# Expert choice in a fused decoder layer: logits and ranks out of PSUM by ScalarE, the choice in four steps

## The chip, the cores and the metric

One core of one Trainium2 chip runs the whole kernel. The metric is device time in microseconds (us) of one execution; the median of 3 runs before the change is 750.56 us (749.78 to 751.29).

## The reference, cut to what matters

The layer takes 64 sequences of 64 tokens, 128 wide, all float32, and adds three blocks one after the other, each on a layer norm of what came before:

```python
x = x + self_attention(layernorm(x))            # 16 heads of 8, causal
x = x + cross_attention_and_ffn(layernorm(x), ctx)
x = x + ffn_block(layernorm(x))                 # below
# ffn_block: h = x + rotary_attention(rmsnorm(x)); y = h + moe(rmsnorm(h))
logits = xf @ w_router                          # 4096 x 8
probs = softmax(logits); topw, topi = top_k(probs, 2)
topw = topw / sum(topw)
out = sum over the two chosen experts of topw * (silu(xf @ wg) * (xf @ wu)) @ wd
```

The change touches what lies between the logits and the sorted rows: for each token the first and the second best of 8 experts, their two weights, and the row of each (token, expert) pair in an array sorted by expert.

## The kernel before, in words

**Jobs.** The 4096 tokens are 8 tiles of 512, each of 4 sub-tiles of 128 (`SUB`). Each tile goes through three kinds of job, SELF, CROSS and ROTARY, in an order given by `JOBS` (line 123): 24 jobs, of which the ROTARY ones are jobs 11, 14, 16, 18, 20, 21, 22 and 23. A job is four slots, one for each pair of sequences, written (n, p) below. `walk` (line 185) is the order of the work on every engine. In slot (n, p) come, in this order:

- scores (TensorE, L950 and L962) and their shift by the row maximum (VectorE, `shift_scores`, L1145 the maximum, L1149 the subtraction) for the *next* slot;
- the steps of the first half slot, "place 0";
- `attend` (TensorE, L990) and `normalise` (VectorE, L1159 and L1161) for the slot before;
- the transposes of the shifted scores (TensorE, L974) and the exponentials (ScalarE, L1019) of (n, p);
- the steps of the second half slot, "place 1".

**Steps.** What surrounds attention is cut into named steps, and `STEPS` (line 131) lists by hand, for a job n+away, in which slot and half slot of job n each stands. Away 2 and 1 are steps before the job's attention (st, ap: norm; xT, q, k, v: transposes and projections, qr and kr their rotated halves), -1 those behind it (oT, wo, h0, h1, ff, and for ROTARY st2, ap2, hT), -2 and -3 the routing of a ROTARY job: `lg` (logits), `rk` (ranks) and `s0` to `s3`, the moves of the four sub-tiles. Each engine walks the same list and does its own part of each step, strictly in that order; where two jobs have steps in one half slot, the one with the lower away comes first. What is left after the last job is in `last_steps` (line 168).

**The routing before.** `lg`: TensorE makes the logits (L921, slot 0, place 1 of job n-away). VectorE's `choose_dve` (line 444) waits for them, copies them out of PSUM (L453), and chooses in a chain of dependent small instructions (L457 to L463: maximum, less than it, index or 8, first index, one-hot, for both choices), gives the logit gap (L465) and sums up choices (`carried`, L466 to L469). `rk`, one slot later: TensorE sums ranks (L925, L926) once `sel_ready` is there; ScalarE turns the gap into a weight (L1071); VectorE's `place_dve` (line 475) reads the ranks from PSUM (L482), makes row numbers and weights (L485 to L494), and releases the moves by `rows_known`. Each move is two indirect DMAs issued by GpSimd (L1331), which also runs the norm factors (`layer_norm`, `rms`, L1272), the two rotary sums (L1339 for kr, L1341 for qr) and two passes of ap2 (L1322, L1325), all in one queue.

**PSUM.** All these products go through a ring of four banks (`BANKS`). The use number c of a bank, counted over steps, transposes and attends in the order of `walk`, waits until use c-4 has been drained (`free`, line 867), so an engine that copies a bank out late holds up TensorE four uses later. The names of uses are in `count_uses` (line 219).

**The expert stage.** After the last step VectorE makes tables (`tables_dve`), and 71 blocks of 128 sorted rows go through the experts. SyncE loads the first block only after all moves have landed (`rows_moved`, line 555).

## Time and profile before

| | |
|---|---|
| median of 3 runs | 750.56 us |
| the profiled execution | 752.07 us, its span 750.3 us |
| mean granted TensorE clock | 0.915 of full speed |
| attention stage, 28 to 534 us of the span | 24 jobs of 4 slots |
| moves and tables alone, 534 to 568 us | GpSimd issues 22 of the 64 indirect DMAs |
| experts and the sum, 568 us to the end | 71 blocks |

The spans of a busy engine say little here: TensorE, VectorE, ScalarE and GpSimd hand work to each other in every slot. The time line has for each entry its start in us, its length in us, engine, line, operation, output and inputs, the count of instructions merged, and in brackets how long the engine sat idle before and what released it. A slot is best told by VectorE: L1145 is the first instruction of each, so a window from one of its starts to the next is one slot.

### The profile page before, as it was taken

How to read it: one execution, taken by the hardware profiler on the slowest of the kernel's cores; microseconds unless marked ns; L12 is line 12 of the kernel's file. 1: busy time of each engine (PE TensorE's matmuls, PEld its weight loads, DVE VectorE, ACT ScalarE, POOL GpSimd, SP SyncE). 2: the span in 40 equal slices, each digit the busy share in tenths (PEclk: the TensorE clock that was granted, in tenths of full speed). 3: DMA queues.
4: the chain of work that ended last, by engine and by line, in shares of the span. 5: the costliest groups of instructions: out<-in, count | busy, mean ns of one | idle time of the engine just before them, and what ended most of it. 6: DMA issues, size and time to landing. Idle time of an engine off the chain costs nothing.

```text
span 750.3 us, 28778 instructions
## 1 busy us (share of the span) xinstructions
PE 617.3 (82%) x11859; PEld 465.6 (62%) x11859; DVE 504.5 (67%) x1165; ACT 376.8 (50%) x742; POOL 250.4 (33%) x361
## 2 busy tenths in 40 slices
PE   3798999999989879988879679687525999999960
PEld 2465766766656656655546446455425999999960
DVE  3377687777777876876777567477652666666645
ACT  4254566556655536464544424423243777667730
POOL 6010110101121324423633442425771444444440
PEclk9599999999999989999999889898756999999995
DMA  4304600001001000100100000000022222222219
GB/s 127 109 18 137 174 18 18 28 17 42 3 21 37 3 26 32 42 17 17 42 19 27 16 23 24 16 17 31 30 64 53 56 69 66 63 65 62 65 51 325
DMA packets 44960, 38.88 MB, mean 52 GB/s; under 512 B 11248, under 2 KB 37424, under 8 KB 44832
## 3 DMA queue, kind: packets, MB, share of 16 engines
q1 hardware_dynamic: 40512, 28.11, 12.7%
q0 software_dynamic: 4320, 8.92, 3.5%
q8 instruction: 97, 1.59, 0.9%
q14 instruction: 31, 0.25, 0.1%
HBM read 18.71 MB, written 12.01 MB: 41 GB/s over the span
## 4 chain that ended last, share of the span: by engine, by line
PE 60%; DVE 17%; issue 7%; POOL 7%; DMA 4%; ACT 4%; SPq 1%; DVEq 0%; POOLq 0%; ACTq 0%
PE ps_s L615 12%; PE ring L937 7%; PE ring L974 7%; PE ps_s L962 6%; DVE rmax L1145 5%; PE ring L623 5%; PE ring L990 5%; DVE shifted L1149 5%; POOL moved_dram L1331 3%; PE ring L860 3%; PE ps_s L950 3%; PE ring L851 3%; PE ring L913 2%; PE ring L917 2%; PE ring L910 2%
## 5 line engine op out<-in xcount | busy, mean ns | idle before, releaser
L1145 DVE TENSOR_REDUCE rmax<-ps_s 128x16 f32<-128x1024 f32 x96 | 117.2, 1221 | 80.3 <-PE ps_s L962 79.9
L1019 ACT ACTIVATE probsT<-ring 128x512 f32<-128x512 f32 x192 | 104.9, 595 | 123.3 <-PE ring L974 123.1
L1149 DVE TENSOR_TENSOR shifted<-ps_s,rmax 128x1024 f32<-128x1024 f32 x96 | 117.6, 1225 | 10.3 <-PE ring L990 0.5
L974 PE MATMUL ring<-const,shifted 128*128 128x128 f32 x768 | 109.1, 286 | 2.7 <-DVE room L1221 2.6
L615 PE MATMUL ps_s<-room 128*128 128x128 f32 x852 | 108.9, 279 | 0.0
L615 PEld LDWEIGHTS ps_s<-room 128*128 128x128 f32 x852 | 102.9, 196 | 0.0
L582 POOL DMA_INDIRECT y_dram<-room x71 | 68.0, 957 | 94.8 <-DVE room L701 92.1
L990 PEld LDWEIGHTS ring<-vbd,probsT 128*32 128x32 f32 x6144 | 64.5, 112 | 55.7 <-issue 53.3
L974 PEld LDWEIGHTS ring<-const,shifted 128*128 128x128 f32 x768 | 85.4, 145 | 7.5 <-DVE room L1221 3.4
L692 DVE SCALAR_TENSOR_TENSOR room<-room,ps_s 128x384 f32<-128x384 f32 x71 | 39.3, 554 | 59.8 <-ACT room L665 59.8
L990 PE MATMUL ring<-vbd,probsT 128*32 128x18 f32 x6144 | 75.0, 188 | 3.7 <-issue 2.6
L653 ACT ACTIVATE room<-w_exp 128x768 f32 x71 | 59.7, 843 | 29.8 <-issue 24.9
L1272 POOL TENSOR_TENSOR pt<-mv,small 128x4 f32<-128x4 f32 x24 | 4.8, 200 | 198.5 <-DVE mv L1174 198.5
L1331 POOL DMA_INDIRECT moved_dram<-moved,pos_i x64 | 62.6, 978 | 24.3 <-issue 15.9
L962 PE MATMUL ps_s<-room,qT 32*64 32x256 f32 x1536 | 68.5, 414 | 2.2 <-DVE shifted L1149 2.2
L623 PE MATMUL ring<-w_exp,room 128*128 x426 | 59.2, 276 | 0.9 <-DVE room L701 0.9
L623 PEld LDWEIGHTS ring<-w_exp,room 128*128 128x128 f32 x426 | 53.3, 192 | 1.1 <-issue 1.1
L937 PE MATMUL ring<-xT,w_f 128*128 128x512 f32 x64 | 37.7, 673 | 13.4 <-ACT xT L1083 10.2
L1058 ACT ACTIVATE vbd<-ring 64x512 f32<-64x512 f32 x48 | 30.4, 633 | 35.1 <-PE ring L860 34.8
L695 DVE TENSOR_TENSOR room<-room,ps_s 128x384 f32<-128x384 f32 x71 | 39.3, 554 | 7.3
L1221 DVE TENSOR_TENSOR room<-ring,const 128x512 f32<-128x512 f32 x32 | 22.0, 686 | 26.5 <-PE ring L937 26.5
L962 PEld LDWEIGHTS ps_s<-room,qT 32*64 32x64 f32 x1536 | 23.0, 134 | 26.9 <-issue 23.7
(159 smaller groups left out, 897.7 us busy)
## 6 DMA issues: line engine op xcount, KB each, us to landing
room<-kS SPq DMA_DIRECT2D x96, 64.0 KB, 1.9
room<-moved_dram SPq DMA_DIRECT2D x71, 65.0 KB
room<-y_dram SPq DMA_DIRECT2D x16, 256.0 KB, 5.7
room<-in_x SPq DMA_DIRECT2D x8, 256.0 KB, 3.5
out<-room SPq DMA_DIRECT2D x8, 256.0 KB, 6.1
cin<-in_ctx SPq DMA_DIRECT2D x8, 192.0 KB, 2.8
w_exp<-in_L_ffn_wg SPq DMA_DIRECT2D x1, 1536.0 KB, 8.6
w_exp<-in_L_ffn_wu SPq DMA_DIRECT2D x1, 1536.0 KB, 11.9
```

What stands on the lines that cost most here:

```text
L582: G.indirect_dma_start(out=y_dram, in_=yb[r], in_offset=None, out_offset=bass.IndirectOffsetOnAxis(ap=xb[r].bitcast(I32)[:, E:E + 1], axis ...
L615: last = mm(bank[r][:, k * P:(k + 1) * P], w, xbT[r], start=True, stop=True)
L623: last = mm(y_bank[r], hh[r][:, k * P:(k + 1) * P], weights(e, W_DOWN + k * E, E), start=(k == 0), stop=(k == HC - 1))
L653: nc.scalar.activation(w_held[c % HELD], w, ACT.Copy).then_inc(w_copied, 1)
L937: last = mm(ps_g[:], w, (cT if kind == CROSS and name == "k" else xT)[:], start=True, stop=True)
L962: last = mm(ps_s[SEQ * b:SEQ * b + SEQ, g], qT[r][some, tok:tok + SEQ], kbd[r][some, :, tok:tok + SEQ], start=not causal, stop=True)
L974: last = nc.tensor.transpose(ring[u.bank][:, k * P:(k + 1) * P], flat[:, c:c + P], ident)
L990: last = mm(ring[u.bank][rows, c:c + 2 * (D + 1)], probsT[p % 2][:, k, rows], vbd[r][:, at:at + 2 * (D + 1)], start=True, stop=True)
L1019: nc.scalar.activation(probsT[p % 2][:, 4 * g:4 * g + 4, :], ring[u.bank][:].rearrange("p (k c) -> p k c", c=P), ACT.Exp, scale=SCALE)\
L1145: V.reduce_max(rmax[p % 2][:].rearrange("p (g k) -> p g k", g=GROUPS), ps_s, AX.X).then_inc(rmax_ready, 1)
L1149: V.tensor_tensor(shifted[p % 2][:].rearrange("p (g k) s -> p g k s", g=GROUPS), ps_s, rmax[p % 2][:].rearrange("p (g k) -> p g k", g=GROU ...
L1331: G.indirect_dma_start(out=moved_dram, in_=moved[t % 2][:, k, s, :], in_offset=None, out_offset=bass.IndirectOffsetOnAxis(ap=pos_i[t % 2][ ...
```

## The change

The choice is taken apart and moved. `lg` and `rk` are now drained by ScalarE, with a copy into SBUF each (`logits`, `rank`, the latter one row of 8 longer in the last tile), and VectorE no longer reads either bank. VectorE's part becomes four steps: `c0` (`choose_dve`: four `max` instructions that give the 8 sorted logits of a sub-tile each, gap, not equal, index or 8), `c1` (`hot_dve`: the one-hot rows of both choices), `c2` (`carry_dve`: sums) and `pl` (`place_dve`). They stand in slot 1 place 0 (c0), slot 1 place 1 (c1, c2) and slot 3 place 0 (pl); `rk` goes from slot 1 to slot 2. The moves go later: s0 from slot 2 to slot 3, s1 from slot 3 to slot 0 of the next job, s2 and s3 from slot 1 place 1 to slot 0 place 1 and slot 1 place 0 of that job. `last_steps` is ordered anew.

```diff
@@ -140,13 +140,14 @@
          ROTARY: (((), ()), (("oT",), ("wo", "st2")), ((), ("ap2",)), ((), ("hT",)))},
     -2: {SELF: (((), ()), ((), ()), ((), ()), ((), ())),
          CROSS: (((), ()), ((), ()), ((), ()), ((), ())),
-         ROTARY: (((), ("lg",)), ((), ("rk",)), ((), ("s0",)), ((), ("s1",)))},
+         ROTARY: (((), ("lg",)), (("c0",), ("c1", "c2")), ((), ("rk",)), (("pl",), ("s0",)))},
     -3: {SELF: (((), ()), ((), ()), ((), ()), ((), ())),
          CROSS: (((), ()), ((), ()), ((), ()), ((), ())),
-         ROTARY: (((), ()), ((), ("s2", "s3")), ((), ()), ((), ()))},
+         ROTARY: ((("s1",), ("s2",)), (("s3",), ()), ((), ()), ((), ()))},
 }
 MOVES = ("s0", "s1", "s2", "s3")
-NOT_ON_PE = ("st", "ap", "ap3", "st2", "ap2") + MOVES
+CHOICE = ("c0", "c1", "c2")
+NOT_ON_PE = ("st", "ap", "ap3", "st2", "ap2", "pl") + CHOICE + MOVES
 
 
 def steps_at(n, p, place):
@@ -168,18 +169,20 @@
 def last_steps():
 
     last = N_JOBS - 1
-    yield "lg", last - 1
-    yield "s2", last - 2
-    yield "s3", last - 2
+    for name in MOVES[1:]:
+        yield name, last - 2
     yield "oT", last
     yield "wo", last
-    yield "rk", last - 1
+    yield "lg", last - 1
     yield "st2", last
     yield "ap2", last
-    for name in MOVES:
+    for name in CHOICE + ("rk", "pl"):
         yield name, last - 1
-    for name in ("hT", "lg", "rk") + MOVES:
+    for name in ("hT", "lg") + CHOICE + ("rk", "pl"):
         yield name, last
+    for n in (last - 1, last):
+        for name in MOVES:
+            yield name, n
 
 
 def walk(steps, scores, shift, attend, exps):
@@ -322,9 +325,10 @@
     ones = sb("ones", [P, P])
     warm = sb("warm", [P, 1])
     logits = sb("logits", [P, SUB, EXPERTS])
-    top = sb("top", [P, 2, SUB])
+    top = sb("top", [P, SUB, EXPERTS])
+    other = sb("other", [P, 2, SUB, EXPERTS])
+    keyed = sb("keyed", [P, 2, SUB, EXPERTS])
     first_at = sb("first_at", [P, 2, SUB])
-    less, keyed, second = [sb(name, [P, SUB, EXPERTS]) for name in ("less", "keyed", "second")]
     chosen = sb("chosen", [P, 2, SUB, EXPERTS])
     sel = sb("sel", [P, SUB, EXPERTS])
     carried = sb("carried", [P, SUB + 1, EXPERTS])
@@ -333,7 +337,7 @@
     pos_i = [sb(f"pos_i{r}", [P, 2, SUB], I32) for r in range(2)]
     gap, w1st, wsum = [sb(name, [P, SUB]) for name in ("gap", "w1st", "wsum")]
     region_at = sb("region_at", [P, EXPERTS])
-    last_row = sb("last_row", [P, EXPERTS])
+    rank = sb("rank", [P, SUB + 1, EXPERTS])
     pad_at = sb("pad_at", [1, EXPERTS], I32)
     counts_i = sb("counts_i", [1, EXPERTS], I32)
     blocks_i = sb("blocks_i", [1, EXPERTS], I32)
@@ -441,28 +445,39 @@
         ins.then_inc(dve_chain, 1)
         dve.wait_ge(dve_chain, chain[0])
 
+    numbers = const[:, C_IOTA:C_IOTA + EXPERTS].unsqueeze(1).broadcast_to([P, SUB, EXPERTS])
+
+    def per_expert(x):
+        return x.unsqueeze(2).broadcast_to([P, SUB, EXPERTS])
+
     def choose_dve(dve, n):
 
         V, t, u = nc.vector, TILE_OF[n], used("lg", n)
-        iota = const[:, C_IOTA:C_IOTA + EXPERTS].unsqueeze(1).broadcast_to([P, SUB, EXPERTS])
-
-        def wide(x):
-            return x.unsqueeze(2).broadcast_to([P, SUB, EXPERTS])
-
-        dve.wait_ge(ring_filled, u.filled())
-        V.tensor_copy(logits[:], ring[u.bank][:, 0:SUB * EXPERTS].rearrange("p (s e) -> p s e", s=SUB))\
-         .then_inc(ring_drained[u.bank], 1)
         dve.wait_ge(ring_drained[u.bank], u.drained())
-        for k, src in enumerate((logits, second)):
-            in_turn(dve, V.reduce_max(top[:, k, :], src[:], AX.X))
-            in_turn(dve, V.tensor_tensor(less[:], src[:], wide(top[:, k, :]), ALU.is_lt))
-            in_turn(dve, V.scalar_tensor_tensor(keyed[:], less[:], float(EXPERTS), iota, ALU.mult, ALU.add))
-            in_turn(dve, V.tensor_reduce(first_at[:, k, :], keyed[:], AX.X, ALU.min))
-            in_turn(dve, V.tensor_tensor(chosen[:, k], iota, wide(first_at[:, k, :]), ALU.is_equal))
-            if k == 0:
-                in_turn(dve, V.scalar_tensor_tensor(second[:], chosen[:, 0], -1e30, logits[:], ALU.mult, ALU.add))
+        for s in range(SUB):
+            last = V.max(out=top[:, s, :], in_=logits[:, s, :])
+        in_turn(dve, last)
         wait(dve, weight_ready, t)
-        V.tensor_tensor(gap[:], top[:, 1, :], top[:, 0, :], ALU.subtract).then_inc(gap_ready, 1)
+        V.tensor_tensor(gap[:], top[:, :, 1], top[:, :, 0], ALU.subtract).then_inc(gap_ready, 1)
+        for k in range(2):
+            last = V.tensor_tensor(other[:, k], logits[:], per_expert(top[:, :, k]), ALU.not_equal)
+        in_turn(dve, last)
+        for k in range(2):
+            last = V.scalar_tensor_tensor(keyed[:, k], other[:, k], float(EXPERTS), numbers, ALU.mult, ALU.add)
+        in_turn(dve, last)
+
+    def hot_dve(dve, n):
+
+        V = nc.vector
+        in_turn(dve, V.tensor_reduce(first_at[:, 0], keyed[:, 0], AX.X, ALU.min))
+        in_turn(dve, V.tensor_tensor(chosen[:, 0], numbers, per_expert(first_at[:, 0]), ALU.is_equal))
+        in_turn(dve, V.scalar_tensor_tensor(keyed[:, 1], chosen[:, 0], float(EXPERTS), keyed[:, 1], ALU.mult, ALU.add))
+        in_turn(dve, V.tensor_reduce(first_at[:, 1], keyed[:, 1], AX.X, ALU.min))
+        in_turn(dve, V.tensor_tensor(chosen[:, 1], numbers, per_expert(first_at[:, 1]), ALU.is_equal))
+
+    def carry_dve(dve, n):
+
+        V, t = nc.vector, TILE_OF[n]
         V.tensor_copy(carried[:, 0, :], region_at[:] if t == 0 else carried[:, SUB, :])
         in_turn(dve, V.tensor_tensor(sel[:], chosen[:, 0], chosen[:, 1], ALU.add))
         for s in range(SUB):
@@ -475,13 +490,9 @@
     def place_dve(dve, n):
 
         V, t, u = nc.vector, TILE_OF[n], used("rk", n)
-        dve.wait_ge(ring_filled, u.filled())
-        rank = ring[u.bank][:, 0:SUB * EXPERTS].rearrange("p (s e) -> p s e", s=SUB)
-        if t == TILES - 1:
-            in_turn(dve, V.tensor_copy(last_row[:], ring[u.bank][:, SUB * EXPERTS:(SUB + 1) * EXPERTS]))
-        V.tensor_tensor(at_expert[:], chosen[:], rank.unsqueeze(1).broadcast_to([P, 2, SUB, EXPERTS]), ALU.mult)\
-         .then_inc(ring_drained[u.bank], 1)
         dve.wait_ge(ring_drained[u.bank], u.drained())
+        in_turn(dve, V.tensor_tensor(at_expert[:], chosen[:], rank[:, 0:SUB, :].unsqueeze(1)
+                                     .broadcast_to([P, 2, SUB, EXPERTS]), ALU.mult))
         in_turn(dve, V.reduce_sum(pos_f[:], at_expert[:], AX.X))
         r = t % 2
         wait(dve, rows_moved[r], MOVED * (t // 2))
@@ -496,8 +507,8 @@
     def tables_dve(dve):
 
         V = nc.vector
-        V.tensor_copy(pad_at[:], last_row[0:1, :]).then_inc(pads_known, 1)
-        in_turn(dve, V.tensor_scalar(counts_i[:], last_row[0:1, :], float(P - 1), None, ALU.add))
+        V.tensor_copy(pad_at[:], rank[0:1, SUB, :]).then_inc(pads_known, 1)
+        in_turn(dve, V.tensor_scalar(counts_i[:], rank[0:1, SUB, :], float(P - 1), None, ALU.add))
         in_turn(dve, V.tensor_scalar(blocks_i[:], counts_i[:], 7, None, ALU.logical_shift_right))
         in_turn(dve, V.tensor_copy(blocks_f[:, 3, :], blocks_i[:]))
         first = const[0:1, C_IOTA:C_IOTA + EXPERTS]
@@ -1066,10 +1077,22 @@
                 apply_rms(n)
             elif name == "ap3":
                 apply_third(n)
-            elif name == "rk":
-                act.wait_ge(gap_ready, TILE_OF[n] + 1)
-                nc.scalar.activation(w1st[:], gap[:], ACT.Exp).then_inc(weight_ready, 1)
-            if name in MOVES or name in ("st", "ap", "ap3", "st2", "ap2", "wo", "ff", "lg", "rk", "qr", "kr") or (kind == ROTARY and name in ("q", "k")):
+            elif name in ("lg", "rk"):
+                u, t = used(name, n), TILE_OF[n]
+                ps = ring[u.bank][:].rearrange("p (s e) -> p s e", e=EXPERTS)
+                if name == "lg":
+                    wait(act, sel_ready, t)
+                    act.wait_ge(ring_filled, u.filled())
+                    nc.scalar.activation(logits[:], ps[:, 0:SUB, :], ACT.Copy).then_inc(ring_drained[u.bank], 1)
+                else:
+                    wait(act, rows_known, t)
+                    act.wait_ge(ring_filled, u.filled())
+                    rows = SUB + 1 if t == TILES - 1 else SUB
+                    nc.scalar.activation(rank[:, 0:rows, :], ps[:, 0:rows, :], ACT.Copy)\
+                      .then_inc(ring_drained[u.bank], 1)
+                    act.wait_ge(gap_ready, t + 1)
+                    nc.scalar.activation(w1st[:], gap[:], ACT.Exp).then_inc(weight_ready, 1)
+            if name in MOVES or name in CHOICE or name in ("pl","st", "ap", "ap3", "st2", "ap2", "wo", "ff", "lg", "rk", "qr", "kr") or (kind == ROTARY and name in ("q", "k")):
                 return
             u = used(name, n)
             if name == "v":
@@ -1193,9 +1216,13 @@
                 u = used("wo", n)
                 dve.wait_ge(ring_drained[u.bank], u.drained())
                 stats_of(NORMS["st2", n], hres)
-            elif name == "lg":
+            elif name == "c0":
                 choose_dve(dve, n)
-            elif name == "rk":
+            elif name == "c1":
+                hot_dve(dve, n)
+            elif name == "c2":
+                carry_dve(dve, n)
+            elif name == "pl":
                 place_dve(dve, n)
             elif name in ("wo", "ff", "qr", "kr") or (kind == ROTARY and name in ("q", "k")):
                 u = used(name, n)
```

## Rows read from the trace of the kernel before

**Rows 1.** The page, part 1: busy time, share of the span, instructions of each engine.

```profile
PE 617.3 (82%) x11859; PEld 465.6 (62%) x11859; DVE 504.5 (67%) x1165; ACT 376.8 (50%) x742; POOL 250.4 (33%) x361
```

**Rows 2.** The waits, whole span: who waited for whom, us in total, times, longest.

```profile
PE ring L913 <- DVE at_expert L482: 10.3, 3, 3.5
...
DVE logits L453 <- PE ring L921: 10.5, 7, 7.1
...
PE ring L910 <- DVE at_expert L482: 7.7, 3, 3.3
```

**Rows 3.** Windows, slots (13,1) (16,1) (18,1) (20,0) (20,1) (21,1) (22,1) (23,1): us, busy us of each engine, PEclk, DMA share, GB/s.

```profile
274.55:283.11 8.56, 5.41 (x81) 4.52 (x84) 4.58 (x15) 1.63 (x5) 1.78 (x5) 0.60 0.01 2
...
339.98:346.71 6.73, 3.57 (x27) 0.99 (x28) 3.88 (x13) 1.84 (x6) 4.73 (x11) 0.75 0.00 0
...
386.82:392.71 5.89, 2.74 (x27) 0.95 (x28) 3.88 (x13) 1.71 (x6) 4.21 (x10) 0.87 0.00 0
...
431.19:441.17 9.98, 8.47 (x188) 5.57 (x188) 8.47 (x34) 3.06 (x6) 2.17 (x2) 1.00 0.08 29
...
441.17:449.76 8.59, 5.44 (x59) 3.01 (x60) 3.87 (x14) 2.35 (x6) 6.47 (x13) 0.60 0.05 17
...
466.67:472.04 5.37, 4.37 (x120) 3.53 (x112) 4.72 (x15) 2.30 (x5) 3.85 (x11) 1.00 0.02 5
...
497.20:505.20 8.00, 5.85 (x92) 4.90 (x96) 5.84 (x21) 1.76 (x5) 1.67 (x3) 0.79 0.00 0
...
519.39:526.75 7.36, 4.82 (x76) 3.37 (x80) 5.76 (x22) 0.30 (x2) 0.00 (x0) 0.60 0.04 11
```

**Rows 4.** Time line of slots 0 and 1 of job 20, VectorE and TensorE.

```profile
435.55 0.19 DVE L453 COPY logits<-ring 128x32 f32<-128x32 f32 x1 [0.72 <-PE ring L921]
...
438.61 0.77 DVE L469 TENSOR_TENSOR carried<-carried,sel 128x8 f32<-128x8 f32 x4
...
441.17 1.19 DVE L1145 TENSOR_REDUCE rmax<-ps_s 128x16 f32<-128x1024 f32 x1
...
443.88 0.29 DVE L1161 TENSOR_TENSOR att<-ring,rden 128x128 f32<-128x128 f32 x1
...
444.32 2.05 PE L913 MATMUL ring<-oT,w 128*128 128x512 f32 x2 [3.25 <-DVE at_expert L482]
...
445.15 0.17 DVE L494 TENSOR_TENSOR moved<-w1st,moved 128x4 f32<-128x4 f32 x1
```

**Rows 5.** Prices: time line of job 20; then instruction groups of VectorE and ScalarE by form.

```profile
440.87 0.38 DVE L1174 BATCH_NORM_AGGREGATE mv<-stats 128x2 f32<-128x6 f32 x4
...
L461 DVE TENSOR_TENSOR chosen<-const,first_at 128x32 f32<-128x32 f32 x16 | 3.1, 192 | 0.6
...
L1125 ACT ACTIVATE bias_qk<-ps_s 128x2 f32<-128x2 f32 x1 | 0.2, 172 | 0.1
```

**Rows 6.** Time line of job 18's end and job 19, GpSimd and ScalarE.

```profile
403.86 1.27 POOL L1339 TENSOR_TENSOR kS<-room 128x512 f32<-128x512 f32 x1 [7.08 <-DVE room L1221]
...
408.97 1.27 POOL L1341 TENSOR_TENSOR qT<-room 128x512 f32<-128x512 f32 x1 [3.84 <-DVE room L1221]
...
419.07 0.95 POOL L1331 DMA_INDIRECT moved_dram<-moved,pos_i  x1 [0.30 <-issue]
...
422.01 1.28 ACT L1049 ACTIVATE moved<-hres,rstd 128x128 f32<-128x128 f32 x4 [3.54 <-POOLq L1277]
```

**Rows 7.** Time line of job 14, GpSimd and TensorE.

```profile
295.71 0.20 POOL L1272 TENSOR_TENSOR pt<-mv,small 128x4 f32<-128x4 f32 x1 [4.53 <-DVE mv L1174]
...
302.69 0.60 PE L851 MATMUL ring<-const,xh 128*128 128x128 f32 x4
```

**Rows 8.** Time line of the last moves, GpSimd.

```profile
526.92 0.19 POOL L1272 TENSOR_TENSOR pt<-mv 128x4 f32<-128x4 f32 x1 [7.78 <-DVE mv L1174]
...
545.49 1.06 POOL L1331 DMA_INDIRECT moved_dram<-moved,pos_i  x1 [0.18 <-issue]
...
564.51 0.96 POOL L1331 DMA_INDIRECT moved_dram<-moved,pos_i  x1 [0.30 <-issue]
```

## The prediction

> **What bounds the kernel now.** I read the page first, then the waits, then slot by slot the time line. TensorE is busy for 82% of the span and VectorE for 67% [rows 1], but neither is simply the limit: the question is who waits in the slots that hold the choice. The waits name it. TensorE stood for 18.0 us in six places ahead of the first product behind oT (L913 and L910), and VectorE for 10.5 us ahead of its copy of the logits [rows 2]. The time line of job 20 shows how they hang together. VectorE waits 0.72 us for the logits, and from 435.55 to 439.38 it does nothing but the choice (3.83 us). So the next row maximum starts only at 441.17, the normalisation behind it ends at 444.17, and TensorE, which needs that normalisation's bank for h0, has stood for 3.25 us [rows 4]. The releaser printed is the read of ranks (L482); by its place in the bank count h0 waits for L1161, which ended 0.15 us before h0 began. After the stall the clock is down: PEclk is 0.60 in slot (20,1), and the two passes of L913 take 2.05 us [rows 3, 4]. Slots (20,0) and (20,1) take 9.98 and 8.59 us; slot (21,1), which has no choice but the same kind of work, takes 5.37 [rows 3].
>
> A second limit is GpSimd. In job 19 it runs norm factors from 410.2 on, then four indirect DMAs to 420.0, and ScalarE waits 3.54 us for the factors behind them [rows 6]. A third is the end: sixteen DMAs in one unbroken row, the first at 545.49, the last at 564.51, so 1.27 us each, and the experts start behind the last [rows 8].
>
> **The change, part by part.**
>
> *The choice itself.* Twelve dependent instructions of VectorE ahead of the sums, about 0.22 us apart (192 ns busy each, and the hand-over) [rows 5], and the gap, become: four max, gap, two unequal, two index-or-8, then five dependent ones. No row shows a max. Four independent small instructions, bn_aggr, took 0.38 us together [rows 5]; four dependent ones 0.77 us [rows 4]. I take 0.4, since the four max are independent too, and keep 0.8 as the upper end; less than 0.4 I exclude, as they are issued one by one. Then c0 is 0.4 + 0.4 + 0.3 = 1.1 us, c1 5 x 0.22 = 1.1, c2 1.1 as now. Together 3.3 us against 3.83, and the wait for the logits moves to ScalarE, where the copy has a nearest row of 172 ns from PSUM [rows 5] and is covered by that engine's idle time (2.35 us busy of the 8.59 of slot (20,1)) [rows 3].
>
> The Trainium skill (VectorE: DVE Perf Modes, section on the TRN2 errata) speaks against four small max: an operation from SBUF pays a fixed latency between instructions, so many small tiles pay it each time; by its formula (N+151)/0.96 ns, four of 8 elements in a row would be an estimated 0.66 us, and the sum below smaller by some 1.6 us. The trace disagrees for bn_aggr, whose 0.38 us leave 95 ns for each.
>
> *Where it stands.* Slot 0 loses the whole block. In job 20 the next maximum can then start when its scores and the stats ahead of it are done, by my working at 438.5, 2.7 us earlier than 441.17 [rows 4]; the same working gives 2.55 for job 13, 2.35 for 22, 2.9 for 16, 18 and 23. Slot 1 gains c0 ahead of the normalisation and c1, c2 behind it, and loses the placing (1.2 us, from the end of L1161 at 444.17 to that of L494 at 445.32). Maximum, shift and normalisation take 3.0 us (441.17 to 444.17) [rows 4], with a hand-over 3.1; + 1.1 + 2.2 makes 6.4. VectorE is busy in slot (13,1) 0.7 us longer than in (20,1), where it adds wo, and in (22,1) 2.0 longer, for hres and its stats [rows 3]. So slot 1 becomes 7.1 in job 13 (8.56 now), 6.4 in 16, 18 and 20 (6.73, 5.89, 8.59), 8.4 in 22 and 23 (8.00, 7.36) [rows 3]. With slot 0 that is 4.0 us for job 13, 3.2 for 16, 2.4 for 18, 4.9 for 20, 1.95 for 22 and 1.9 for 23.
>
> That holds where VectorE is last. h0 or wo no longer shares a bank with the normalisation, as the ranks' use of the ring has gone one slot on: it starts right behind the transposes; v, one use later, still waits. In 16 and 18 TensorE, late and at a lowered clock (PEclk 0.75 and 0.87) [rows 3], was behind VectorE at the next job's scores and gains more, 4.0 and 3.95. In 20 the ranks and xT, now ahead of these scores on TensorE, limit it to 3.3, in 13 the copies of xh and cT on ScalarE to 3.5. **Gain 3.5 + 4.0 + 3.95 + 3.3 + 1.95 + 1.9 = 18.6 us.**
>
> *pl in slot 3, place 0.* Eight instructions, 1.2 us, now stand ahead of the drains of ff and k or of a normalisation; q or kr waits for these banks. By the distance of the uses, 0.85 in job 13, 0.9 in 16, 0.7 in 18, 0.6 in 22; in job 20 0.35, the rest hidden in the wait for factors that follows anyway. **Cost 3.4.**
>
> *The moves in GpSimd's queue.* s1 and s2 (four DMAs, 5.1 us) now stand ahead of qr and of the norm factors of st, in jobs 14, 17, 19 and 21, and only s3 between these and st2. In job 19 GpSimd idles 3.84 us ahead of qr [rows 6], which takes up most of it; the factors come some 2.5 us later, but st2's come where they were, as its queue holds six DMAs and less idle time in place of four, and ScalarE's wait of 3.54 us [rows 6] stays. So 17, 19 and 21 cost nothing beyond what is counted. In job 14 there is no qr and the moves start only after pl: six DMAs at 1.27, 7.6 us, from about 291.5 (my estimate for the end of pl) to 299.1, against a start of the factors at 295.71; the transposes of xT at 302.69 [rows 7] slip by 2.25 us, of which 0.85 was counted. **Cost 1.4.** SyncE's queue has no move in it and keeps its order. Between nothing and the full 5.1 us a job I keep both ends for the range.
>
> *The end.* s1(21) to s3(21) start when pl(21) is done, at about 529.3, as now at 529.7, and GpSimd stays full from there; st2(22), from which that chain hangs (526.92) [rows 8], is earlier by the 1.9 counted. ScalarE copies the ranks of job 22 behind ap2(23), so its rows are known 0.8 us after GpSimd is ready for them. The choice of job 23 is some 2 us ahead of its moves and costs nothing. **Cost 0.8.**
>
> **Sum:** 18.6 - 3.4 - 1.4 - 0.8 = 13.0 us. The profiled execution took 752.07 us, 1.77 outside its span, so it would be 739.1; it lies 1.51 above the median, so the forecast for the median is **737.6 us**. A measurement of this kernel can tell about 0.2%, 1.5 us.
>
> **The rivals.**
>
> *A, half is given back.* The factors of st come 2 to 3 us late in four jobs, ScalarE waits in its own order in front of the exponentials, and TensorE behind these. For it: ScalarE already waited for factors in job 19 [rows 6]. Against it: two of the four jobs have ScalarE busy until then. At 1.6 us in four jobs: 13.0 - 6.4 = 6.6, so 744.0 us.
>
> *B, the stall in front of st2 shrinks as well.* If the earlier moves fill the gap ahead of qr (3.84) [rows 6] and TensorE's clock, once held up, stays up through slots 1 and 2, then jobs 19 and 21 give about 1.5 us each and the clock 3 more: 731.6 us.
>
> *C, slower: the queue of GpSimd.* Its place is slot 0 of jobs 14, 17, 19 and 21; its price the whole of four DMAs, 5.07 us, if the rows become known too late to use the idle time. It decides when more than (13.0 + 1.4) / 4 = 3.6 us a job come through to TensorE; at 5.07 the sum is 13.0 + 1.4 - 20.3 = -5.9, so 756.5 us. Against it: the idle time of 3.84 to 4.53 us is there [rows 6, 7].
>
> *D, no change.* The change doesn't unload what TensorE waits for: c0 ahead of the normalisation and c1, c2 ahead of the drain of wo cost slot 1 what slot 0 gains. Then only the shorter choice counts, six times 0.5 = 3.0, less than the costs of 5.6 but within the accuracy of these; 751 us. Against it: the wait for L1161 is lifted from h0 and wo by the bank count alone.
>
> **How the numbers follow.** Forecast 0.47, A 0.24, B 0.14, C 0.08, D 0.07. The forecast's own spread is 3 us either way (0.4 us more for max in six jobs is 2.4; each job's gain to 0.5). The range runs from 731 (B) to 746 (A with the dearer max), leaving out C, D and a part of B. Faster by over 0.2%: 0.47 + 0.24 + 0.14 and a little of D, 0.86; the same 0.06; slower 0.08.
>
> **What would show it.** Right: slot 0 of jobs 13, 16, 18 and 20 shorter by 2.4 to 2.9 us; no wait of L913 or L910 for VectorE over 1 us; PEclk near 1 in slot 1; the last move starting some 13 us earlier than 564.51; four max in about 0.4 us. Wrong, by step: a wait of L1031 for GpSimd of several us in jobs 14 to 21 (A, C); L1049's wait of 3.54 us gone (B); slot 1 longer than 8.4 us, or wo still stalled (D); a gap in the last sixteen moves of more than 1 us.

## The result and the profile after

The changed kernel takes **742.76 us** (median, 739.68 to 746.7, 7 runs) where the kernel before, on the same chip, takes 750.57 (749.78 to 752.77, 7 runs). The ratio is 0.9895, interval 0.9867 to 0.9923: 7.8 us faster. The profiled execution took 740.64 us, its span is 738.8. A second set of the same kernel is `again` below. The forecast of 737.6 was on the right side and 5 us too low; 742.76 lies in its range of 731 to 746.

In the kernel after, a line of VectorE's slot code is 23 higher than before: the row maximum is L1168, the normalisation L1182 and L1184. h0 is L924, wo L921, v L871, the scores' first product L961, ScalarE's copies L1086 (logits) and L1091 (ranks), the moves L1358.

The page, part 1 (busy time, share, instructions), answers to [rows 1]: nearly the same work in 11.5 us less.

```profile
PE 611.1 (83%) x11859; PEld 464.1 (63%) x11859; DVE 503.0 (68%) x1172; ACT 379.6 (51%) x758; POOL 250.2 (34%) x361
```

The waits, whole span (who, for whom, us in total, times, longest), answer to [rows 2]:

```profile
POOL moved_dram L1358 <- DVE moved L505: 51.1, 7, 12.8
...
PE ring L871 <- DVE att L1184: 12.4, 8, 2.5
ACT moved L1060 <- POOLq L1304: 10.7, 6, 2.5
...
ACT xh L1042 <- POOLq L1304: 8.2, 3, 4.9
```

Of the 18.0 us of h0 and wo, 0.7 is left; v (L871) waits 12.4 us in shorter pieces, where before the change it waited 6.3. The first line is new in its size (0.3 us before): GpSimd stands for the placing of the rows (L505).

Windows of the same slots as [rows 3], (13,1) (16,1) (18,1) (20,0) (20,1) (21,1) (22,1) (23,1), same columns:

```profile
272.30:279.06 6.76, 4.27 (x91) 3.48 (x94) 6.21 (x27) 2.35 (x4) 1.78 (x5) 1.00 0.01 2
336.96:343.16 6.20, 5.86 (x170) 3.50 (x170) 5.65 (x24) 4.94 (x10) 2.28 (x8) 1.00 0.01 3
382.37:388.57 6.20, 5.86 (x170) 3.50 (x170) 5.65 (x25) 4.93 (x10) 2.30 (x8) 1.00 0.01 3
426.00:433.26 7.26, 6.60 (x170) 4.10 (x173) 5.27 (x14) 2.06 (x6) 2.17 (x2) 1.00 0.11 40
433.26:439.78 6.52, 4.35 (x95) 2.87 (x84) 5.71 (x27) 3.09 (x6) 3.59 (x10) 1.00 0.01 3
458.29:463.67 5.38, 4.38 (x121) 3.54 (x113) 4.72 (x16) 2.31 (x5) 4.34 (x10) 1.00 0.05 15
483.25:491.82 8.57, 6.96 (x215) 5.92 (x215) 7.53 (x33) 3.37 (x6) 1.09 (x1) 1.00 0.02 5
504.19:512.43 8.24, 6.38 (x184) 5.09 (x183) 7.55 (x33) 3.06 (x7) 4.72 (x5) 1.00 0.16 51
```

PEclk (the third figure from the end) is 1.00 in every one, where it was 0.60 to 0.87 in most of them before. VectorE is busy for 5.71 of the 6.52 us of slot (20,1), and TensorE waits for it there (below): VectorE now sets that slot.

The time line of slot (20,1) answers to [rows 4]:

```profile
433.26 1.19 DVE L1168 TENSOR_REDUCE rmax<-ps_s 128x16 f32<-128x1024 f32 x1
433.43 1.09 PE L985 MATMUL ring<-const,shifted 128*128 128x128 f32 x8
...
434.36 1.02 PE L924 MATMUL ring<-oT,w 128*128 128x512 f32 x2
...
435.70 0.36 DVE L458 MAX8 top<-logits 128x8 f32<-128x8 f32 x4
...
437.12 0.29 DVE L1184 TENSOR_TENSOR att<-ring,rden 128x128 f32<-128x128 f32 x1
...
437.56 1.15 PE L871 MATMUL ring<-w_f,xT 128*64 128x64 f32 x32 [2.17 <-DVE att L1184]
...
438.74 0.77 DVE L484 TENSOR_TENSOR carried<-carried,sel 128x8 f32<-128x8 f32 x4
```

h0 (L924) has no bracket: it starts right behind the transposes and takes 1.02 us, not 2.05. The wait is now in front of v, 2.17 us. The four max take 0.36.

The same clock of slots can be laid over both traces. All times are us, slots named as in the prediction:

| job | 13 | 16 | 18 | 20 | 22 | 23 | sum |
|---|---|---|---|---|---|---|---|
| slot 0, before | 9.98 | 8.48 | 8.48 | 9.98 | 8.72 | 6.69 | 52.3 |
| slot 0, after | 7.27 | 5.61 | 5.59 | 7.26 | 6.35 | 3.84 | 35.9 |
| slot 1, before | 8.56 | 6.73 | 5.89 | 8.59 | 8.00 | 7.36 | 45.1 |
| slot 1, after | 6.76 | 6.20 | 6.20 | 6.52 | 8.57 | 8.24 | 42.5 |
| slot 2, before | 4.47 | 4.15 | 4.98 | 4.18 | 3.75 | | 21.5 |
| slot 2, after | 5.35 | 4.54 | 5.41 | 4.92 | 4.41 | | 24.6 |
| slot 3, before | 3.74 | 6.01 | 6.01 | 6.35 | 3.75 | | 25.9 |
| slot 3, after | 4.11 | 7.60 | 6.88 | 7.22 | 4.12 | | 29.9 |

So slots 0 and 1 gave 19.05 us; slots 2 took 3.1 of it back and slots 3 took 4.1, together 7.2. Job 14's slots 0 and 2 took another 2.6. Slots (19,3) and (21,3), which hold the wait for the factors of st2, went from 12.04 to 9.69 and from 12.68 to 9.49: 5.5 more gained. Start-up and the other slots took 0.5. At the last slot VectorE is 14.3 us ahead.

Some 4 us of these are lost in the tail. GpSimd's time line there, answering to [rows 8]:

```profile
512.60 0.19 POOL L1299 TENSOR_TENSOR pt<-mv 128x4 f32<-128x4 f32 x1 [2.48 <-DVE mv L1197]
...
517.38 1.06 POOL L1358 DMA_INDIRECT moved_dram<-moved,pos_i  x1 [0.88 <-DVE moved L505]
...
535.14 1.06 POOL L1358 DMA_INDIRECT moved_dram<-moved,pos_i  x1 [3.60 <-DVE moved L505]
...
554.16 0.96 POOL L1358 DMA_INDIRECT moved_dram<-moved,pos_i  x1 [0.30 <-issue]
```

The head is 14.3 us earlier (526.92 to 512.60) and the last move 10.35. The gap of 3.60 us in front of s0(22) is nearly all of the difference. From there to the end 1.2 us came back.

### The profile page after: what moved, and what is told of

It is laid out like the page before. It is cut to its first block, busy times and chain, and to the rows that moved or that the text cites. A ratio compares the mean times of both kernels' runs of the same rounds, so it can differ in the third digit from the quotient of the medians.

```text
span 738.8 us, 28821 instructions
## 1 busy us (share of the span) xinstructions
PE 611.1 (83%) x11859; PEld 464.1 (63%) x11859; DVE 503.0 (68%) x1172; ACT 379.6 (51%) x758; POOL 250.2 (34%) x361
## 4 chain that ended last, share of the span: by engine, by line
PE 58%; DVE 16%; issue 11%; POOL 7%; ACT 4%; DMA 2%; SPq 0%; DVEq 0%; POOLq 0%; ACTq 0%
PE ps_s L626 13%; PE ring L985 7%; PE ring L948 7%; PE ring L634 6%; PE ps_s L973 6%; DVE rmax L1168 5%; PE ring L1001 5%; DVE shifted L1172 4%; POOL moved_dram L1358 3%; PE ring L871 3%; PE ring L862 3%; PE ps_s L961 2%; PE ring L928 2%; POOL rstd L1299 1%; PE ring L921 1%
## 5 line engine op out<-in xcount | busy, mean ns | idle before, releaser
L1168 DVE TENSOR_REDUCE rmax<-ps_s 128x16 f32<-128x1024 f32 x96 | 117.2, 1221 | 77.6 <-PE ps_s L973 77.0
L1358 POOL DMA_INDIRECT moved_dram<-moved,pos_i x64 | 62.6, 978 | 70.3 <-DVE moved L505 51.1
L1069 ACT ACTIVATE vbd<-ring 64x512 f32<-64x512 f32 x48 | 30.4, 633 | 30.5 <-PE ring L871 30.3
L973 PEld LDWEIGHTS ps_s<-room,qT 32*64 32x64 f32 x1536 | 22.7, 132 | 26.6 <-issue 23.4
```

The lines of the kernel that those rows point to most:

```text
L973: last = mm(ps_s[SEQ * b:SEQ * b + SEQ, g], qT[r][some, tok:tok + SEQ], kbd[r][some, :, tok:tok + SEQ], start=not causal, stop=True)
L1168: V.reduce_max(rmax[p % 2][:].rearrange("p (g k) -> p g k", g=GROUPS), ps_s, AX.X).then_inc(rmax_ready, 1)
L1358: G.indirect_dma_start(out=moved_dram, in_=moved[t % 2][:, k, s, :], in_offset=None, out_offset=bass.IndirectOffsetOnAxis(ap=pos_i[t % 2][ ...
```

## The experiments

Each ran beside the kernel before, whose median was 750.57 us in the first set (again, old_places, moves_late_pair, tail), 750.02 in the second (lump_slot0, lump_slot1, pl_slot2, pl2_tail) and 749.3 in the third (the rest). The intervals of the ratios are 0.2 to 0.4% wide to either side, so a difference of 2 us between two sets is not told apart from none. All edits are to the changed kernel unless another is named. The rows of `STEPS` and `last_steps` are all that most of them touch.

### again: the changed kernel once more

> The changed kernel once more, as it is. Its runs so far lie between 739.7 and 746.7 us, those of before between 749.8 and 752.8. Expected: a median of 742.8 within 1.5 us, again with a spread of several us. If the spread comes from the attention stage (one theory), the start of the last move in this trace differs from 554.2 us by as much as the time does from 740.6; if it comes from the expert stage (the other), the last move stays at 554.2 within 0.5 us and the rest differs.

741.48 us (738.99 to 742.29), ratio 0.9888 (0.9866 to 0.991). This is the number the others are held against. Its last move starts at 551.93, 2.2 us sooner than above, with 1.65 us less of time, so the difference does not come from the expert stage; but it doesn't come from the slots either: the very first row maximum starts at 26.32 and not at 28.45. The profile shows how far two executions of one kernel differ: slots (12,3) and (13,1) took 5.61 and 8.17 us, in the profile above 6.79 and 6.76, and slot (2,1), long before any routing, took anything from 4.9 to 10.4 us over these runs. A difference of 2 us between two single profiles means nothing unless its slot is named.

### old_places: copies and shorter choice, old places

```diff
-ROTARY: (((), ("lg",)), (("c0",), ("c1", "c2")), ((), ("rk",)), (("pl",), ("s0",)))
+ROTARY: (((), ("lg", "c0", "c1", "c2")), ((), ("rk", "pl")), ((), ("s0",)), ((), ("s1",)))
-ROTARY: ((("s1",), ("s2",)), (("s3",), ()), ((), ()), ((), ()))
+ROTARY: (((), ()), ((), ("s2", "s3")), ((), ()), ((), ()))
```

> ScalarE's copies of logits and ranks and the shorter choice (four max) as in the changed kernel, but every step in the half slot where it stood before (choice behind lg in slot 0, ranks and placing in slot 1, moves and the last steps as before). If the gain comes from where the steps stand, little is left: a choice shorter by 0.5 us in six jobs, less 0.2 us for the hand-over from ScalarE, 1 to 3 us in all, so 748 to 750 us, with L1145's equivalent wait and the stall of the first product behind oT back at about 3 us each. If it comes from the copies or the max themselves, 743 us.

748.34 us, ratio 0.997 (0.9951 to 0.9989). Slots (20,0) and (20,1) are 9.76 and 8.71 us, as before the change. In the old places the new instructions are worth 2.2 us (0.8 to 3.7 by the interval); the other 7 are the places.

### lump_slot0, lump0_rk2 and lump_slot1: the choice's place against the ranks' place

```diff
 # lump_slot0
+ROTARY: (((), ("lg", "c0", "c1", "c2")), ((), ("rk",)), ((), ()), (("pl",), ("s0",)))
 # lump0_rk2
+ROTARY: (((), ("lg", "c0", "c1", "c2")), ((), ()), ((), ("rk",)), (("pl",), ("s0",)))
 # lump_slot1
+ROTARY: (((), ("lg",)), (("c0", "c1", "c2"), ()), ((), ("rk",)), (("pl",), ("s0",)))
```

> The scores (lg) and all of the choice stand together in slot 0, place 1; ranks in slot 1, place 1; the planned positions (pl) and s0 stay in slot 3. Theory 1 (the gain comes from what slot 1 loses): slot 0 takes the 3.3 us of the choice behind its normalisation, where VectorE would have to wait for ScalarE's copy of the scores as well, and slot 1 of the six jobs loses another 1.1 us; the sum of both slots is the same or up to 1 us worse for each job: 742 to 748 us. Theory 2 (VectorE has room in slot 0, whose length PE and GpSimd set): each of the six jobs is another 0.5 to 1 us shorter, 735 to 738 us.

> lump_slot0 (757.1 us) with one edit: the ranks go from slot 1 to slot 2, so that one use of the ring fewer lies between the normalisation's bank and h0 or wo. In lump_slot0 TensorE waited 3.25 us ahead of h0 in slot 1 of job 20 for a normalisation that had no choice ahead of it. Theory 1 (the bank count makes h0 wait): h0 starts right behind the transposes, and v, one use later, takes over about 2.1 us of the wait at a higher clock; 1 to 2 us less in each of jobs 13, 16, 18, 20, 22: 747 to 752 us. Theory 2 (only VectorE's work ahead of the row maximum counts, the bank does not): 755 to 758 us.

> All of the choice (c0, c1, c2) stands in slot 1 ahead of the normalisation, as before the change; ScalarE keeps both copies out of PSUM, and the moves stay where the change put them. Theory 1 (the split pays because c1 and c2 no longer stand between PE's scores and the normalisation): c1 and c2 are 2.2 us of VectorE, so slot 1 of jobs 13, 16, 18, 20, 22 and 23 is as long as it was or up to 2 us longer than after the change, where the slot of 20 and 22 holds the wait for the second half's statistics and hides part of it. Six times 1 to 2 us, some of it given back in the tail: 5 to 9 us over the changed kernel, 746 to 750 us. Theory 2 (VectorE's total is what counts, its places do not): nothing is added and nothing taken away, so the time is the changed kernel's within 1 us, 740 to 743 us. The old_places run, with all of the change but the places, stood at 748.3, and does not tell the choice's places from those of the moves and of the ranks; this run does.

| kernel | choice in | ranks in | median us | slots 0 + 1 of six jobs |
|---|---|---|---|---|
| lump_slot0 | slot 0 | slot 1 | 757.13 | 51.0 + 47.7 |
| lump0_rk2 | slot 0 | slot 2 | 743.46 | 50.9 + 28.7 |
| changed (again) | slot 1, split | slot 2 | 741.48 | 35.9 + 43.8 |
| lump_slot1 | slot 1, ahead of the normalisation | slot 2 | 750.66 | 35.9 + 51.5 |

The first pair differs in the place of the ranks alone, and by 13.7 us. In lump_slot0 no choice stands in slot 1, yet h0 waits there as it did before the change. Its time line, slot (20,1), and then that of lump0_rk2:

```profile
449.00 0.29 DVE L1184 TENSOR_TENSOR att<-ring,rden 128x128 f32<-128x128 f32 x1
449.44 2.05 PE L924 MATMUL ring<-oT,w 128*128 128x512 f32 x2 [3.25 <-DVE att L1184]
```

```profile
440.88 1.02 PE L924 MATMUL ring<-oT,w 128*128 128x512 f32 x2
...
441.50 1.19 DVE L1168 TENSOR_REDUCE rmax<-ps_s 128x16 f32<-128x1024 f32 x1
...
444.23 0.29 DVE L1184 TENSOR_TENSOR att<-ring,rden 128x128 f32<-128x128 f32 x1
444.67 1.15 PE L871 MATMUL ring<-w_f,xT 128*64 128x64 f32 x32 [2.77 <-DVE att L1184]
```

In the second, h0 has started before VectorE's slot has begun (440.88 against 441.50), and only v waits. The kernel's own count of uses (`count_uses`) says why: with the ranks in slot 1, the fourth use ahead of h0 is the attend that the normalisation drains, and with the ranks gone it is oT; v comes behind the attend instead. The windows of slot (20,1), lump_slot0 first (length, busy times, PEclk):

```profile
446.28:455.15 8.87, 5.71 (x59) 3.01 (x60) 2.87 (x6) 2.71 (x8) 3.60 (x10) 0.62 0.01 2
```

```profile
441.50:446.88 5.38, 2.61 (x58) 1.59 (x58) 2.88 (x6) 1.87 (x4) 3.59 (x10) 1.00 0.00 0
```

TensorE's stand and the lowered clock go together: 0.62 with the wait of 3.25 us, 1.00 with 2.77 behind a busy h0. Theory 1 of lump0_rk2 was right in kind and low in size: 743.46 against 747 to 752, and h0's wait had cost more than the 1 to 2 us a job put on it: slots (16,1) and (18,1) fell by 3.2 to 3.3 us each. The ranks are not free where they went: the five slots 2 grew from 21.7 to 23.5 us. Both theories of lump_slot0 missed: 757.13 against at most 748, since neither counted the wait of h0 that came back.

With the ranks in slot 2, moving the choice from slot 0 to slot 1 only moves 15 us from one slot to the other, 79.7 against 79.8 in the sum, and the medians, 743.46 and 741.48 in different sets, are not told apart. What matters within slot 1 is what stands ahead of the normalisation. In lump_slot1 it is all of the choice:

```profile
443.26 0.77 DVE L484 TENSOR_TENSOR carried<-carried,sel 128x8 f32<-128x8 f32 x4
...
444.67 1.98 PE L871 MATMUL ring<-w_f,xT 128*64 128x64 f32 x32 [4.27 <-DVE att L1184]
```

v waits 4.27 us, then takes 1.98 us and not 1.15. That costs 2.4 to 3.8 us in (13,1), 3.6 in (20,1) and 1.6 in (22,1), and nothing in 16, 18 and 23. Together 8 to 9 us in three jobs, where theory 1 had 5 to 9 in six; theory 2 falls. So the move into slot 1 needs the split, or it costs 9 us; with the split it is even with leaving the choice in slot 0.

### copy_by_dve: VectorE copies the logits

```diff
-        dve.wait_ge(ring_drained[u.bank], u.drained())
+        dve.wait_ge(ring_filled, u.filled())
+        V.tensor_copy(logits[:], ring[u.bank][:, 0:SUB * EXPERTS].rearrange("p (s e) -> p s e", s=SUB))\
+         .then_inc(ring_drained[u.bank], 1)
+        dve.wait_ge(ring_drained[u.bank], u.drained())
...
-                    nc.scalar.activation(logits[:], ps[:, 0:SUB, :], ACT.Copy).then_inc(ring_drained[u.bank], 1)
```

> The changed kernel, but VectorE copies the logits out of PSUM, at the head of c0 in slot 1, place 0; ScalarE keeps the copy of the ranks. Theory 1 (ScalarE's copy is what allows the choice to stand a slot later): the bank of the logits is held until c0, and the fourth use behind it, the transposes of slot 1, waits for it. In job 20 they started at 433.4 and c0 at 435.7, so 2.3 us and more for each of six jobs, some of it behind the row maximum that is due in any case: 748 to 757 us. Theory 2 (the copy is only an instruction of 0.2 us that changes engines): six times 0.25 us over the changed kernel, 742 to 743.5 us.

742.05 us (740.32 to 744.6): not told apart from the changed kernel, as theory 2 had it. Yet the wait that theory 1 named is there, in slot (20,1):

```profile
438.94 0.18 DVE L457 COPY logits<-ring 128x32 f32<-128x32 f32 x1
...
439.27 1.84 PE L988 MATMUL ring<-const,shifted 128*128 128x128 f32 x8 [2.52 <-DVE logits L457]
...
442.75 1.16 PE L874 MATMUL ring<-w_f,xT 128*64 128x64 f32 x32
```

The transposes wait 2.52 us for the bank, and v (here L874) no longer waits: TensorE stands once in front of a VectorE that is late anyway. Slot (20,1) grew by 1.95 us, those of 16, 18 and 23 by 0.2 each. In this trace the tail gave as much back: from GpSimd's first factor of the tail to the last move it took 39.1 us, in the changed kernel 41.6. So the copy of the logits by ScalarE, by itself, has no effect that the medians show. The copy of the ranks was not tested alone.

### pl_slot2: the placing behind the ranks

```diff
-((), ("rk",)), (("pl",), ("s0",))
+((), ("rk", "pl")), ((), ("s0",))
```

> The planned positions (pl) go from slot 3, place 0, where they stand ahead of the normalisation, to slot 2, place 1, right behind the ranks. Theory 1 (pl in slot 3 costs what the slot tables showed: some 3.9 us less 2.0 for the moves in job 14, 1.6 to 2.0 in job 16, less in the others): the slots named become shorter by 1.5 to 2 us in jobs 13 and 16 and by 0.5 in 18, 20 and 22, and slot 2 of each grows by up to 0.6 us where VectorE waits for ScalarE's copy of the ranks: 2 to 4 us faster than the changed kernel, 737 to 739.5 us. Theory 2 (a wait for the copy of the ranks holds up the residual sum behind it in slot 2, as pl is now due right behind PE's ranks): 0.5 to 1.2 us more in each slot 2, no gain or a loss of up to 3 us, 741 to 745 us.

734.25 us, ratio 0.9801 (0.9766 to 0.9837): some 7 us faster than the changed kernel, and nearly 3 below theory 1's range. The slots 3 of the five jobs fall from 29.9 to 26.6 us, the slots 2 stay (24.6 and 24.8), and job 14 gets its 2.6 back. GpSimd's wait for the placing falls from 51.1 to 30.4 us. GpSimd and ScalarE from slot (13,3) into job 14, in the changed kernel and then here:

```profile
288.42 1.20 POOL L1358 DMA_INDIRECT moved_dram<-moved,pos_i  x1 [6.34 <-DVE moved L505]
...
295.95 0.21 POOL L1299 TENSOR_TENSOR pt<-mv,small 128x4 f32<-128x4 f32 x1
...
300.13 1.65 ACT L1042 ACTIVATE xh<-room,shift,rboth 128x128 f32<-128x128 f32 x4 [2.48 <-POOLq L1304]
```

```profile
282.30 1.20 POOL L1358 DMA_INDIRECT moved_dram<-moved,pos_i  x1 [2.07 <-DVE moved L505]
...
291.36 0.20 POOL L1299 TENSOR_TENSOR pt<-mv,small 128x4 f32<-128x4 f32 x1 [1.53 <-DVE mv L1197]
...
295.54 1.65 ACT L1042 ACTIVATE xh<-room,shift,rboth 128x128 f32<-128x128 f32 x4
```

The six DMAs (three moves) are as long in both; above, the factors start straight behind them and ScalarE waits, below they are done 1.53 us before the factors start.

### moves_late_pair and moves_half_up: where the moves stand

```diff
 # moves_late_pair
+ROTARY: (((), ("lg",)), (("c0",), ("c1", "c2")), ((), ("rk",)), (("pl",), ("s0", "s1")))
+ROTARY: (((), ()), ((), ("s2", "s3")), ((), ()), ((), ()))
 # moves_half_up, an edit to pl2_tail below
+ROTARY: (((), ("lg",)), (("c0",), ("c1", "c2")), ((), ("rk", "pl")), (("s0",), ("s1",)))
+ROTARY: ((("s2",), ("s3",)), ((), ()), ((), ()), ((), ()))
```

> As the changed kernel, but s0 and s1 both in slot 3 and s2, s3 in slot 1 place 1 of the next job as before, so that no move stands ahead of qr and of the norm factors. If the moves ahead of the factors cost more than they give (rival A of the prediction), the slots of job 14 (14,1 to 15,0: 18.6 us in the changed kernel, 16.7 before) get about 2 to 4 us shorter and nothing else longer: 739 to 741 us. If they also take work out of the wait for st2's factors in jobs 19 and 21, as the shorter slots (20,1) and (22,1) of the changed kernel suggest (9.7 and 9.5 us against 12.0 and 12.7), these grow by 2.4 to 3.2 us each and the sum is 743 to 746 us.

> pl2_tail (731.55 us) with every move a half slot or more earlier: s0 and s1 in slot 3, places 0 and 1, s2 and s3 in slot 0 of the next job, places 0 and 1. Theory 1 (moves cost where they stand ahead of something due in GpSimd's queue, and slot 1 of the next job, with the rotary sum and the factors of st2 behind it, is such a place): 729 to 731 us. Theory 2 (s0 directly behind pl holds GpSimd's queue until the rows are known, in slot 3, where the norm factors and the rotary sum of kr stand behind it): 1 to 2 us more in jobs 17, 19 and 21, 733 to 737 us.

moves_late_pair: 741.87 us, the changed kernel's time, between the two theories; both their slots are there. Job 14 got 2.0 us back, though pl still stands in slot 3, but slots (19,3) and (21,3) became 11.82 and 12.47 us against 9.69 and 9.49, so the early moves are what had shortened them. moves_half_up: **724.58 us** (721.83 to 725.43), ratio 0.9654 (0.9626 to 0.9682), 7.0 below pl2_tail; the same two slots are 6.21 and 6.16 us, in pl2_tail 9.91 and 10.44. Theory 1 was right in kind and 4 us too small. GpSimd, ScalarE and TensorE in job 19, pl2_tail and then moves_half_up:

```profile
401.84 1.28 POOL L1370 TENSOR_TENSOR qT<-room 128x512 f32<-128x512 f32 x1
...
408.05 1.04 POOL L1360 DMA_INDIRECT moved_dram<-moved,pos_i  x1 [0.89 <-POOL shift L1301]
...
412.36 1.28 ACT L1062 ACTIVATE moved<-hres,rstd 128x128 f32<-128x128 f32 x4 [2.12 <-POOLq L1306]
...
414.17 1.35 PE L950 MATMUL ring<-xT,w_f 128*128 128x512 f32 x2 [3.37 <-ACT xT L1108]
```

```profile
403.35 1.28 POOL L1370 TENSOR_TENSOR qT<-room 128x512 f32<-128x512 f32 x1
...
411.64 1.27 ACT L1062 ACTIVATE moved<-hres,rstd 128x128 f32<-128x128 f32 x4
...
413.45 1.12 PE L950 MATMUL ring<-xT,w_f 128*128 128x512 f32 x2 [1.14 <-ACT xT L1108]
```

From qr to ap2 it is 10.5 us with a move (two DMAs) between the two sets of factors, and 8.3 without, and ScalarE waits no more. TensorE's wait for the projection behind it falls by 2.2 us, and its granted clock, 0.83 in slot (19,3) and 0.67 in (21,3) of pl2_tail, is 1.00 in both slots here; neither theory had the clock.

### tail, pl2_tail and c0_early

```diff
 # tail: last_steps
     for name in MOVES[1:]: yield name, last - 2
+    yield "lg", last - 1
+    for name in CHOICE: yield name, last - 1
     yield "oT", last
     yield "wo", last
-    yield "lg", last - 1
+    yield "rk", last - 1
     yield "st2", last
     yield "ap2", last
-    for name in CHOICE + ("rk", "pl"): yield name, last - 1
+    yield "pl", last - 1
 # pl2_tail: pl_slot2 and tail together
 # c0_early: pl2_tail, and
+ROTARY: (((), ("lg", "c0")), ((), ("c1", "c2")), ((), ("rk", "pl")), ((), ("s0",)))
```

> As the changed kernel, but after the last slot the logits and the choice of job 22 stand ahead of oT and wo of job 23, and its ranks ahead of st2. In the changed kernel GpSimd idles 3.6 us ahead of s0 of job 22, since the ranks wait for a choice that stands behind the stats of job 23. If that gap sets the end of the moves, it shrinks to about 1 us and the last move starts 2 to 3 us sooner than 554.2: 740 to 741 us median. If the experts are held by something else (tables, weights), the gap shrinks and the time stays at 742.8.

> Both edits together: pl in slot 2, and in the tail the choice of job 22 ahead of job 23's output projection. If they are independent the gains add: the tail alone was 3 us faster than the changed kernel, so under theory 1 of the pl run 734.5 to 737 us, and under theory 2 738 to 742 us. If the earlier end of pl(22) or of the moves makes the tail's order worth less, the time is that of the better one alone, 737 to 739 us.

> pl2_tail (731.55 us) with c0 half a slot earlier, at the end of slot 0 behind the copy of the logits. In job 20 of lump_slot1 VectorE stood 1.75 us in that place, so 1.1 us of c0 fit into it but for 0.35 us, and in slot 1 the normalisation, for which v waits 2.17 us, comes 1.1 us earlier. Theory 1 (v's wait is what slot 1 costs): 0.5 to 1 us less a job in jobs with that idle time, 728 to 731 us. Theory 2 (what stands ahead of the next row maximum costs in full, as the choice did before the change): 1 us more in each slot 0 and 1 us less in some of slots 1: 731.5 to 735 us.

tail: 738.55 us, ratio 0.9854 (0.9831 to 0.9877), 2.9 below `again` and 1.5 below the range that was expected; s0(22) starts at 531.28 with no gap. pl2_tail: 731.55 us, ratio 0.9751 (0.9722 to 0.9781), 2.7 below pl_slot2, and lower than expected: the gains add, so the two edits are independent. c0_early: 729.06 us (726.37 to 730.93), ratio 0.9725 (0.9698 to 0.9752), another 2.5 (2.0 by the ratios, whose intervals overlap, so the step is not clear of noise). It lies in theory 1's range, and the slots say the same: slots 0 grow by 2.3 in the sum and slots 1 shrink by 7.2. That profile is of its fastest execution, 5.8 us below pl2_tail's, 1.8 of it before the first slot, so it shows more than the medians. c0_early and moves_half_up weren't tried together.

## Why the prediction was right, and where it was wrong

**The choice itself**: right. Four max took 0.36 us, where 0.4 was taken and less excluded; ScalarE's copies took 0.20. The formula that the Trainium skill states (VectorE: DVE Perf Modes, TRN2 errata) had given an estimated 0.66; the four max, issued with no wait between them, took little more than half of that.

**Where it stands**: for slots 0 and 1 right, 18.6 forecast and 19.05 measured (17.7 in `again`). Slot 0 came out 2.71, 2.87, 2.89, 2.72, 2.37 and 2.85 us shorter, each within 0.2 of the forecast; slot 1 came within 0.4. The four corrections that the prediction then made, job by job, are not in these slots: it had 4.0, 3.2, 2.4 and 4.9 us from the slot lengths for jobs 13, 16, 18 and 20 and changed them to 3.5, 4.0, 3.95 and 3.3, while 4.5, 3.4, 2.6 and 4.8 were measured. They cancel in the sum, which was luck. And the reason was put in the wrong order. The prediction credited what slot 0 loses and gave the bank count as a condition; the runs show that the ranks' slot is worth 13.7 us with the choice left in slot 0, and that the choice's move on top of it is not told apart from nothing.

**The ranks in slot 2**: the term that the sum lacks. It charges job 20 for them, within the corrections above, and no other; slots 2 grew in all five, by 3.1 us together (2.8 in `again`, and 2.2 in `tail`, whose edit lies behind the last slot). They are 21.7 us in lump_slot0, with the ranks in slot 1, and 24.8 in pl_slot2, so it is the ranks' place and not that of pl. Part of it is the same count of uses that freed h0: the ranks' use now stands between the attend and xT, so that xT, and no longer ff behind it, waits for the normalisation. Slot (16,2), before and after:

```profile
349.53 0.60 PE L851 MATMUL ring<-const,xh 128*128 128x128 f32 x4
```

```profile
346.35 0.63 PE L862 MATMUL ring<-const,xh 128*128 128x128 f32 x4 [1.90 <-DVE att L1184]
```

In lump0_rk2, where VectorE has no choice in slot 1, the same product does not wait.

**pl in slot 3**: right in size. 3.4 us were counted; slots 3 grew by 4.1, by 3.6 in `again` and by 3.3 in `tail`, and pl_slot2 gives 3.4 back.

**The moves**: 1.4 counted for job 14, 2.6 measured. The 0.6 in slot (14,0) is there in every run with pl in slot 3 and in no other. The 2.05 in slot (14,2) takes both the late start and six DMAs in a row: it goes when pl starts them earlier (pl_slot2), and also when pl stays and only four stand there (moves_late_pair). That st2's factors stay where they were in job 19 was wrong: ScalarE's wait fell from 3.54 to 2.09 us and slot (19,3) by 2.35; (21,3) by 3.19. This was rival B's place, and it gave 5.5 us where B had 3. B's other part, 3 us for the clock, can't be told apart from it: PEclk rose from 0.72 and 0.73 to 0.82 in these two slots, and is 1.00 in the slots 0 and 1 that are in the windows.

**The end**: 0.8 counted, 4.0 measured, of the costs that were counted the one furthest off; the gap of 3.60 us is one of the signs of being wrong that the prediction listed. The text named ScalarE's copy of the ranks; what was late is VectorE, which goes from st2 of job 23 to the choice of job 22:

```profile
527.57 0.37 DVE L458 MAX8 top<-logits 128x8 f32<-128x8 f32 x4
...
529.84 1.13 DVE L481 COPY carried<-carried 128x8 f32<-128x8 f32 x1
...
531.10 1.06 DVE L484 TENSOR_TENSOR carried<-carried,sel 128x8 f32<-128x8 f32 x4
532.21 0.64 PE L936 MATMUL ring<-sel,const 128*128 128x32 f32 x2 [5.44 <-DVE carried L484]
...
533.37 0.20 ACT L1091 ACTIVATE rank<-ring 128x32 f32<-128x32 f32 x1 [2.51 <-PE ring L937]
```

ScalarE copied 0.1 us after TensorE was done. The sum of the profiled pair is then 19.05 + 5.5 - 7.2 - 2.6 - 0.5 - 4.0 + 1.2 = 11.45, and the spans differ by 11.5, against the 13.0 forecast. The medians differ by 7.8 and 9.1. The prediction took off the 1.5 us by which its profiled execution was slower than the median; that of the changed kernel was 2.1 faster than its own. So of the 5 us by which the forecast missed the median, 1.5 are its terms, which err both ways, and the rest is which executions were profiled.

**Rivals.** A's 744.0 is nearer in number than the forecast, but its mechanism, ScalarE standing for late factors in four jobs, shows only in job 14 (2.48 us). C had the right queue, but in jobs 17, 19 and 21 nothing of the four DMAs' price came through; what GpSimd's queue cost is in job 14. D fell: h0 and wo are no longer held up. Its sum, 3.0 less 5.6, would have given 753 and not 751; old_places shows that the copies and the shorter choice are 2.2 us, near its 3.0. What D gave as the point against itself, the bank count, was the main thing.

## What to carry to other kernels

Count the uses of a ring between a product and the drain that it waits for; putting one small step a slot later can take a wait off the path, and was worth more here than moving or shortening the work that seemed to cause it. Then count again in the slot where the step lands: here it put one in front of another product, and the slots 2 grew by 3.1 us. When a step is postponed, price not only its own time but who stands in a queue for it: here GpSimd's in job 14, 2.6 us against 1.4, and the end, 4.0 against 0.8. And test the places of a change one by one: of this one's, the ranks' slot paid, the choice's move was even, the placing's slot and the order of the tail cost, and with those two mended and the moves half a slot up the kernel takes 724.58 us.

## What the runs showed of the hardware that was not expected

A VectorE instruction between SBUF operands can be held while GpSimd runs a tensor operation. The COPY of L481, 0.17 us elsewhere, took 1.13 at 529.84, and at_expert (L494), 0.22 us elsewhere, took 0.65 at 515.36. GpSimd's own lines:

```profile
514.65 1.27 POOL L1349 TENSOR_TENSOR room<-hres,room 128x512 f32<-128x512 f32 x1 [0.18 <-POOL rstd L1299]
...
529.68 1.26 POOL L1349 TENSOR_TENSOR room<-hres,room 128x512 f32<-128x512 f32 x1 [0.18 <-POOL rstd L1299]
```

Both VectorE instructions end within 0.1 us of GpSimd's. `again` has the same two (1.12 and 0.64 us), and in pl2_tail the same at_expert took 0.63 and 0.65 us in the two places where it met this instruction. The shift, the reciprocal and the normalisation at 513.73 to 515.44, each with an input in PSUM, kept their 1.23, 0.25 and 0.29 us beside it. The COPY's hold put 0.96 us on the chain of the tail. The Trainium skill (SBUF — State Buffer, section "Who interferes with whom") states that the two share a port pair held by one instruction at a time, that a VectorE operation with two SBUF inputs or a copy in one of the fast two-port modes needs it, and one with at most one SBUF input outside these modes does not. The trace agrees for the at_expert and for those that read PSUM; whether the COPY ran in such a mode it does not show. In pl2_tail the COPY no longer meets GpSimd's instruction, and takes its usual 0.17 us. No run kept all else the same, so the cause rests on these coincidences.
